# Constants as VectorE row sums, and a new order of the first loads, in a fused perceiver layer

## The chip, the cores and the metric

The kernel runs on one core of a Trainium2 chip, as one launch. The metric is the device time of one execution in microseconds. TensorE (PE) does the matrix products, VectorE (DVE), ScalarE (ACT) and GpSimd (POOL) work on rows, and SyncE (SP) issues nearly all transfers from HBM. The five engines run their own instruction lists in order and meet only at semaphores.

## The reference

For 16 sequences of 64 latent rows `x` (width 512) and 16 contexts of 1,601 key rows (width 384), all float32, one layer is computed:

```python
x = x + xattn(layernorm(x), ctx)      # one head, q = ln(x)Wq+bq, k = ln(ctx)Wk+bk, v = ln(ctx)Wv+bv, softmax, Wo, bo
x = x + attn(layernorm(x), ...)       # 16 heads of 32 on the 64 rows, relative positions
x = x + ffn(layernorm(x), ...)        # W1, W2 ternary by their mean magnitude, exact gelu, 2048 wide
```

Both layernorms of the cross attention have gains and offsets, so that its weights can be multiplied together ahead of the data.

## The kernel before

Two sequences share the 128 partitions, so there are 8 pairs. The work is a pipeline over steps `n`: in step `n` the cross attention of pair `n` is finished and the scores of pair `n+1` are made, self attention of pair `n-1` begins and of pair `n-2` ends. The feed-forward part follows behind all pairs. Every engine's list is written out by hand; what is placed earlier in a list is issued earlier, and a waiting instruction holds all behind it.

What matters here is the start, up to the first pair's output.

- **The fold.** Queries and keys need not be formed: `wqk` = Wq times Wk is made once by 16 products (line 744), 385 columns wide: 384 for the weights, one for the key offset. VectorE prepares the rows of Wk (lines 1212 to 1219), one block `e` of four after the other.
- **Constants.** A vector `TV` of 512 numbers (VectorE, lines 1266 to 1268) is multiplied by the prepared Wk on TensorE as 16 products of one column each (lines 1013 and 1015). `a_rows` (line 772) makes from the turned `x` what the keys are multiplied with; `scores` (line 824) does that for the four chunks 0, 1, tail (3) and 2 of a pair.
- **Key statistics.** VectorE's `key_stats` (line 1241) takes mean and variance of every key row from a second copy of the keys, `nat`, which comes in six loads of two tiles (0 to 5) and a tail of 65 rows. GpSimd raises them to the power of -1/2 (line 414), ScalarE spreads them (line 537), TensorE turns them (`key_factors`, line 797), VectorE multiplies scores by them and takes the maximum (line 1283, `exp_bias` up to line 1294), and ScalarE takes the exponentials (line 550).
- **The value side.** `value_product` makes Wv times Wo (`xwvo`, line 1031, three row blocks `m` of four products), `value_bias` (line 1048) makes a constant row from a vector `SV` (VectorE, lines 1420 and 1422) by four products, and `value_mean` (line 1040) the weighted mean row of `xwvo` by three. VectorE's `value_center` (line 1428) takes that mean off.
- **Weighted keys.** `turn_probs` (line 900), VectorE's `pt_scale` (line 1301) and `weighted` (line 914) go over 13 tiles of the pair. When a tile is used up, SyncE may load the next pair's `nat` into its place (line 274). The sum is turned (line 944), multiplied by `xwvo` (`xattn_o`, line 961) and added to `x` (`x1_sum`, line 1371); after the norm (`x1_norm`, line 1380) `y_turn` (line 1000) follows on TensorE, and then the last scores of the next pair.

On TensorE step 0 begins like this:

```python
                key_factors(p)
                if n == 0:
                    value_product()
                    value_bias()
```

and ends, between the weighted keys and the next pair's scores, with `value_mean()`. On VectorE the list after `exp_bias(0)` is `value_dots()`, `x_stats(1)` and `pt_scale(0, 0)`. On SyncE the first loads are followed by one quarter of the self-attention ("dense") weights `aw`, the next pair's keys and some rows; `step(0)` then waits for `value_bias` (line 348) and loads the other three quarters before any `nat` of pair 1.

Of the kernel before, what the change touches and what calls it, by code (L numbers as in the profile page):

```python
# [16 lines left out]
def build_program(nc, A, out):  # L17
# [25 lines left out]
    with ctx:  # L43
# [44 lines left out]
        wqk, at = carve(at, [P, KD, DC + 1])  # L88
# [14 lines left out]
        wkT, at = carve(at, [P, KE, DC + 1])  # L103
# [23 lines left out]
        xvo_bias, _ = carve(GS_AT + 4096, [P, D])  # L127
        rsk, at = carve(at, [P, H, L])
        ptT, at = carve(at, [P, HP, P])
# [137 lines left out]
        def _(sp):  # L267
# [61 lines left out]
            sp.dma_start(wo, A["wo"]).then_inc(s["wvo_loaded"], 16)  # L329
# [12 lines left out]
            def step(n):  # L342
                wms, following = magnitudes(n), magnitudes(n + 1)
                more = n + 1 < NT
                if n == 0:
                    sp.wait_ge(s["vbias_ps"], 1)
                    for i in range(1, 4):
                        sp.dma_start(aw[i], A["aw"][i]).then_inc(s["dense_loaded"], 16)
                for k in range(NG + 1):
                    if more:  # L350
                        load_nat(n + 1, k)
                    if k in (1, 3, NG) and (1, 3, NG).index(k) + 2 < len(wms):
                        load_wm(wms[(1, 3, NG).index(k) + 2])
                if n + 2 < NT:
                    load_x(n + 2)
# [149 lines left out]
        def _(act):  # L505
            act.wait_ge(s["vec_loaded"], 16)
            for c in range(KD):
                act.wait_ge(s["wqk_ps"], c + 1)
                act.activation(wqk[:, c, :], S[c][:, 0:DC + 1], ACT.Identity, bias=0.0, scale=col("xattn_ln1_g", c)).then_inc(s["wqk_ready"], 1)
# [22 lines left out]
            def spread_factors(p, g):  # L532
# [5 lines left out]
                         rs[p % 2][0:m, 8 * g:8 * g + 2 * n].unsqueeze(2).to_broadcast([m, 2 * n, L])).then_inc(s["factors_spread"], 1)  # L538

# [89 lines left out]
            yTx_out(0)  # L629
# [15 lines left out]
            def step(n):  # L645
# [6 lines left out]
                if n == 0:  # L652
                    for m in range(KC):
                        act.wait_ge(s["xvo_ps"], m + 1)
                        act.copy(xwvo[:, m, :], S[m]).then_inc(s["xvo_taken"], 1)
# [80 lines left out]
        def _(pe):  # L736
# [3 lines left out]
            for e in range(KE):  # L740
                pe.wait_ge(wq_loaded[e], 16)
                pe.wait_ge(s["k_ready"], e + 1)
                for c in range(KD):
                    ins = pe.matmul(S[c][:, 0:DC + 1], wqT[:, e, c * P:(c + 1) * P], wkT[:, e, :], start=(e == 0), stop=(e == KE - 1))
                    if e == KE - 1:
                        ins.then_inc(s["wqk_ps"], 1)
# [261 lines left out]

            x_turn(0)
            pe.wait_ge(s["t_ready"], 1)  # L1010
            for m in range(KC):
                for e in range(KE):
                    pe.matmul(W[0][:, m:m + 1], wkT[:, e, m * P:(m + 1) * P], sm(TV + e), start=(e == 0), stop=(e == KE - 1))
            for e in range(KE):
                ins = pe.matmul(W[0][:, KC:KC + 1], sm(TV + e).to_broadcast([P, P]), wkT[:, e, DC:DC + 1], start=(e == 0), stop=(e == KE - 1))
            ins.then_inc(s["const_ps"], 1)
            bias_max()
# [7 lines left out]
            def value_product():  # L1025
# [3 lines left out]
                for m in range(KC):  # L1029
# [4 lines left out]
            def value_mean():  # L1034

                pe.wait_ge(s["xvo_taken"], KC)
                pe.wait_ge(s["g2d_ready"], 1)
                pe.wait_ge(s["chunk_scaled"], 4)
                for m in range(KC):
                    ins = pe.matmul(S[3], sm(G2D + m).to_broadcast([P, P]), xwvo[:, m, :], start=(m == 0), stop=(m == KC - 1))  # L1040
                ins.then_inc(s["center_ps"], 1)

            def value_bias():

                pe.wait_ge(s["sv_ready"], 1)
                pe.wait_ge(s["chunk_scaled"], 1)
                for e in range(KE):
                    ins = pe.matmul(W[0][:, :], sm(SV + e).to_broadcast([P, P]), wo[:, e, :], start=(e == 0), stop=(e == KE - 1))
                ins.then_inc(s["vbias_ps"], 1)

            def step(n):
                p, t, r = stages(n)
                more = p + 1 < NT
                if t is not None:
                    q_rows(t)
                key_factors(p)
                if n == 0:
                    value_product()
                    value_bias()
# [8 lines left out]
                weighted(p, 1)  # L1068
                turn_probs(p, 3)
# [101 lines left out]
        def _(dve):  # L1171
            for u in range(2):
                dve.memset(st[u], 1.0).then_inc(s["padding_set"], 1)
            dve.wait_ge(s["rows_loaded"], 16)
# [93 lines left out]
            dve.tensor_tensor(sm(TV, KE), sm(TV, KE), col("xattn_bq", 0, KE), ALU.add).then_inc(s["t_ready"], 1)  # L1268
            dve.tensor_scalar(sm(KSC, KD), col("attn_bk", 0, KD), DH ** -0.5, None, ALU.mult).then_inc(s["ksc_ready"], 1)
# [145 lines left out]
            def value_dots():  # L1415
# [6 lines left out]
                dve.tensor_tensor(sm(SV, KE), sm(SV, KE), col("xattn_bv", 0, KE), ALU.add).then_inc(s["sv_ready"], 1)  # L1422

# [7 lines left out]
            def step(n):  # L1431
# [14 lines left out]
                if more:  # L1446
                    x_stats(p + 1)
                pt_scale(p, 0)
# [157 lines left out]
```

## Time and profile before

| what | us |
|---|---|
| median of three runs | 566.79 |
| the three runs | 562.96, 566.79, 568.53 |
| the profiled execution | 566.35 |
| its span, first to last instruction | 564.6 |

The span of the profiled execution is 1.75 us shorter than its time; the rest lies around it. All stages below are read in that one execution, in microseconds from the start of the span. A float32 product appears in the trace as two records, so that 16 products are "x32".

### The profile page before, as it was taken

What the parts mean: (1) busy time and instruction counts of PE and PEld (TensorE: products, weight loads), DVE (VectorE), ACT (ScalarE), POOL (GpSimd) and SP (SyncE); (2) the same over time, 40 slices, a digit from 0 to 9 for tenths busy, and PEclk for the clock granted to TensorE, in tenths of its full rate; (3) what the DMA queues carried; (4) which work ended last, traced back from release to release, by engine and by line L of the source; (5) the groups of instructions that cost most, each with busy time, mean ns of one, the idle gap of its engine ahead of it and who ended that gap; (6) DMA issues with size and microseconds to landing.
All of it is one profiled execution on the core that took longest, in us unless ns stands there. A gap on an engine that the chain in (4) does not pass through costs nothing.

```text
span 564.6 us, 10435 instructions
## 1 busy us (share of the span) xinstructions
PE 525.6 (93%) x4171; PEld 301.9 (53%) x4171; DVE 342.0 (61%) x765; ACT 196.1 (35%) x455; POOL 193.2 (34%) x132
## 2 busy tenths in 40 slices
PE   4979988987999989999998999999988879999996
PEld 2834446553765845666484575656574334444442
DVE  6754185373768468377575836967596895435333
ACT  0233014433723541653373255145143542211110
POOL 0141213224316233440721524269364991000000
PEclk9989999998999999999999999999999989999999
DMA  8999895498499789959959986853527420002002
GB/s 278 424 375 423 330 357 217 184 343 274 174 390 245 276 301 236 324 204 367 262 208 391 202 330 227 241 184 154 113 75 192 145 74 1 1 0 75 0 2 75
DMA packets 42096, 122.45 MB, mean 217 GB/s; under 512 B 19640, under 2 KB 21432, under 8 KB 37312
## 3 DMA queue, kind: packets, MB, share of 16 engines
q1 hardware_dynamic: 24256, 109.20, 53.5%
q10 hardware_dynamic: 17792, 12.58, 9.6%
q8 instruction: 33, 0.54, 0.4%
q14 instruction: 15, 0.12, 0.1%
HBM read 111.29 MB, written 10.49 MB: 216 GB/s over the span
## 4 chain that ended last, share of the span: by engine, by line
PE 61%; DVE 11%; DMA 8%; issue 8%; POOL 5%; ACT 4%; SPq 2%; ACTq 0%; DVEq 0%; POOLq 0%
PE u_ps L914 11%; PE s_ps L1147 9%; PE w_ps L1132 8%; DMA area<-in_kt_dram 6%; PE s_ps L824 6%; PE u_ps L835 5%; PE w_ps L937 5%; POOL area L414 2%; PE w_ps L846 2%; PE w_ps L928 2%; DVE area L1241 2%; PE s_ps L1031 2%; DMA area<-in_nat_dram 2%; PE w_ps L900 1%; DVE area L1325 1%
## 5 line engine op out<-in xcount | busy, mean ns | idle before, releaser
L1241 DVE BATCH_NORM_STATS2 area<-area 128x6 f32<-128x384 f32 (+1 forms) x208 | 99.7, 546 | 26.8 <-DMA area<-in_nat_dram 26.8
L824 PE MATMUL s_ps<-area 128*64 128x512 f32 (+1 forms) x384 | 72.8, 522 | 5.8 <-DMA area<-in_kt_dram 4.8
L914 PE MATMUL u_ps<-area 128*64 128x384 f32 (+1 forms) x416 | 72.4, 491 | 1.2 <-DVE area L1301 1.2
L1147 PE MATMUL s_ps<-area 128*128 128x512 f16 x256 | 61.7, 385 | 4.8 <-DVE area L1520 4.8
L1132 PE MATMUL w_ps<-area 128*128 128x512 f16 x256 | 60.7, 378 | 0.2 <-ACT area L724 0.2
L449 POOL TENSOR_SCALAR area<-area 128x512 f16<-128x512 f32 x32 | 55.6, 1753 | 15.0 <-DMA area<-in_wf_dram 15.0
L414 POOL TENSOR_TENSOR area<-area 128x16 f32<-128x16 f32 (+1 forms) x16 | 39.0, 2438 | 46.6 <-DVE area L1256 46.6
L1283 DVE CUSTOM_DVE_ANT_0 area<-w_ps,area 128x512 f32<-128x512 f32 x24 | 15.4, 690 | 58.6 <-PE w_ps L797 51.8
L724 ACT ACTIVATE area<-w_ps,area 128x512 f32<-128x512 f32 x32 | 22.0, 686 | 79.5 <-PE w_ps L1132 74.0
L824 PEld LDWEIGHTS s_ps<-area 128*64 128x64 f32 x384 | 24.1, 139 | 44.9 <-issue 40.6
L914 PEld LDWEIGHTS u_ps<-area 128*64 128x64 f32 (+1 forms) x416 | 27.6, 135 | 34.2 <-issue 29.5
L1147 PEld LDWEIGHTS s_ps<-area 128*128 128x128 f16 x256 | 24.9, 98 | 37.1 <-DVE area L1520 5.8
L419 POOL TENSOR_TENSOR area<-area 128x1 f32<-128x1 f32 x16 | 9.3, 583 | 92.7 <-DVE area L1363 92.7
L1132 PEld LDWEIGHTS w_ps<-area 128*128 128x128 f16 x256 | 24.3, 96 | 31.1 <-issue 1.0
L1301 DVE TENSOR_TENSOR area<-w_ps,area 128x512 f32<-128x512 f32 (+1 forms) x32 | 18.7, 588 | 34.7 <-PE w_ps L900 34.7
L1518 DVE TENSOR_SCALAR area<-area 128x512 f16<-128x512 f32 x24 | 11.7, 488 | 44.8 <-ACT area L724 44.8
L391 POOL TENSOR_TENSOR area<-area 128x1 f32<-128x1 f32 x8 | 4.4, 553 | 86.0 <-DVE area L1229 86.0
L835 PEld LDWEIGHTS u_ps<-area 128*128 128x128 f32 x256 | 29.2, 191 | 6.7 <-issue 5.7
L835 PE MATMUL u_ps<-area 128*128 128x128 f32 x256 | 30.7, 277 | 0.7 <-ACT area L622 0.7
L846 PE MATMUL w_ps<-area 128*128 128x128 f32 x256 | 30.6, 277 | 0.0
L937 PE MATMUL w_ps<-area 128*128 128x512 f32 x64 | 29.3, 600 | 0.7 <-ACT area L580 0.7
L1412 DVE SCALAR_TENSOR_TENSOR area<-area 128x512 f16<-128x512 f32 x32 | 26.5, 869 | 4.8 <-PE u_ps L914 3.2
(169 smaller groups left out, 835.9 us busy)
## 6 DMA issues: line engine op xcount, KB each, us to landing
area<-in_nat_dram SPq DMA_DIRECT2D x48, 768.0 KB, 10.3
area<-in_kt_dram SPq DMA_DIRECT2D x24, 1536.0 KB, 7.8
area<-in_wf_dram SPq DMA_DIRECT2D x32, 256.0 KB, 8.2
skew<-area ACTq DMA_DIRECT2D x8, 1024.0 KB, 8.6
area<-in_wf_dram SPq DMA_DIRECT2D x16, 512.0 KB, 3.4
area<-in_aw_dram SPq DMA_DIRECT2D x4, 1024.0 KB, 9.3
area<-skew ACTq DMA_DIRECT2D x16, 256.0 KB, 12.2
area<-in_x_dram SPq DMA_DIRECT2D x8, 256.0 KB, 10.2
```

Of the source, the lines that this page charges most:

```text
L414: pool.tensor_tensor(rs[p % 2][:, sl], ve[:, sl], minus_half[:, 0:sl.stop - sl.start], ALU.pow).then_inc(s["rs_ready"], 1)
L449: pool.tensor_scalar(wneg[f % 4][:, w, :], wraw[f % 4][:, w, :], sm(WNTHR + w), None, ALU.is_lt).then_inc(s["neg_done"], 1)
L724: act.activation(gf[i % 2], HID[i % 2][:, :], ACT.Gelu, bias=col("ffn_b1", i % KF), scale=1.0).then_inc(s["gelu_done"], 1)
L824: ins = pe.matmul(S[ch][u * L:(u + 1) * L, 0:n], a_sb[:, c, u * L:(u + 1) * L], x[:, u, c, :], start=(c == 0), stop=(c == KC - 1))
L835: ins = pe.matmul(U[:, m * P:(m + 1) * P], awq[:, c, m * P:(m + 1) * P], yT[:, c, :], start=(c == 0), stop=(c == KD - 1))
L846: ins = pe.matmul(W[0][:, m * P:(m + 1) * P], awk[:, c, m * P:(m + 1) * P], yT[:, c, :], start=(c == 0), stop=(c == KD - 1))
L914: ins = pe.matmul(U[u * L:(u + 1) * L, 0:DC], pT[g % 2][0:m, i, u * L:(u + 1) * L], nat[0:m, j, u, :], start=(j == 0), stop=(j == NJ - 1))
L937: ins = pe.matmul(dst[:, :], ctxT[:, c, :], awo[:, c, :], start=(c == 0), stop=(c == KD - 1))
L1132: ins = pe.matmul(HID[i % 2][:, :], wf16[:, f, 0, c * P:(c + 1) * P], zt[:, 4 * h:4 * h + 4, z, c, :], start=(k == 0), stop=(k == 2 * KD - 1))
L1147: ins = pe.matmul(S[q], g[i % 3][:, q * P:(q + 1) * P], wf16[:, f, 1, :], start=(f == 0 and z == 0), stop=(f == KF - 1 and z == 1))
L1241: dve.bn_stats(st[b][0:m, 2 * j + u, :], nat[0:m, j, u, :]).then_inc(s["key_stats"], 1)
L1412: dve.scalar_tensor_tensor(out=wf16[:, f, w, :], in0=wraw[f % 4][:, w, :], scalar=sm(WTHR + w), in1=wneg[f % 4][:, w, :], op0=ALU.is_gt, o ...
```

## The change

**Sums on VectorE.** The constants, the value bias and the value mean are matrix-vector products whose weights lie on the partitions. Before, TensorE did them in 16, four and three products. Now VectorE multiplies each block by its column of numbers and adds the blocks up (one TENSOR_SCALAR and then SCALAR_TENSOR_TENSORs, each of which waits for the one before), and TensorE sums the one resulting tile over the partitions by a product with ones: four products of one column, one of 512 and one of 512. The three sums lie in `rsk`, which self attention uses later.

**Order on TensorE and ScalarE.** `x` is turned ahead of the fold's last block; two of the three value blocks are made ahead of `key_factors`, the third behind; `value_bias` stands behind the weighted tiles 4 to 7. ScalarE turns out `x` first, takes all four score chunks before it spreads factors, and takes two value blocks out between the first and second half of the factors.

**Order on SyncE.** The first pair's transposed keys `kt` come ahead of most of their second form `nat`; the value weights come ahead of the last `nat`; the three quarters of the dense weights come behind pair 1's `nat`.

**Width.** The fold is 386 columns wide, with one column of zeros (one small memset).

```diff
@@ SyncE, first loads
-            for k in range(2):
-                load_nat(0, k)
             load_kt(0, 0)
+            load_nat(0, 0)
+            load_kt(0, 1)
+            load_nat(0, 1)
+            load_kt(0, NCH)
+            load_kt(0, 2)
             for k in range(2, 4):
                 load_nat(0, k)
-            load_kt(0, 1)
+            sp.dma_start(wvT, A["wvT"]).then_inc(s["wvo_loaded"], 16)
+            sp.dma_start(wo, A["wo"]).then_inc(s["wvo_loaded"], 16)
             for k in range(4, NG + 1):
                 load_nat(0, k)
-            load_kt(0, NCH)
-            load_kt(0, 2)
             load_x(1)
-            sp.dma_start(wvT, A["wvT"]).then_inc(s["wvo_loaded"], 16)
-            sp.dma_start(wo, A["wo"]).then_inc(s["wvo_loaded"], 16)
@@ SyncE, step(0): this block moves behind the loop over load_nat(n + 1, k)
                 if n == 0:
                     sp.wait_ge(s["vbias_ps"], 1)
                     for i in range(1, 4):
                         sp.dma_start(aw[i], A["aw"][i]).then_inc(s["dense_loaded"], 16)
@@ ScalarE
+            act.wait_ge(s["x_turned"], 1)
+            act.copy(yTx.rearrange("p a b -> p (a b)"), W[2][:, :]).then_inc(s["yTx_out"], 1)
...
             scores_out(0, 0)
             key_offset_sums(0)
+            for ch in ORDER[1:]:
+                scores_out(0, ch)
             spread_factors(0, 0)
             spread_factors(0, 1)
-            for ch in ORDER[1:]:
-                scores_out(0, ch)
+            for m in range(KC - 1):
+                value_out(m)
             spread_factors(0, 2)
             spread_factors(0, 3)
@@ TensorE
+            for e in range(KE - 1):
+                fold_qk(e)
             x_turn(0)
-            pe.wait_ge(s["t_ready"], 1)
+            fold_qk(KE - 1)
+            bias_max()
+            pe.wait_ge(s["t_ready"], KE + 1)
             for m in range(KC):
-                for e in range(KE):
-                    pe.matmul(W[0][:, m:m + 1], wkT[:, e, m * P:(m + 1) * P], sm(TV + e), start=(e == 0), stop=(e == KE - 1))
+                pe.matmul(W[0][:, m:m + 1], const_sum[:, m * P:(m + 1) * P], ones_f[:, 0:1], start=True, stop=True)
...
-                for m in range(KC):
-                    ins = pe.matmul(S[3], sm(G2D + m).to_broadcast([P, P]), xwvo[:, m, :], start=(m == 0), stop=(m == KC - 1))
-                ins.then_inc(s["center_ps"], 1)
+                pe.matmul(S[3], ones_f, mean_sum, start=True, stop=True).then_inc(s["center_ps"], 1)
...
+                if n == 0:
+                    value_product(range(KC - 1))
                 key_factors(p)
                 if n == 0:
-                    value_product()
-                    value_bias()
+                    value_product(range(KC - 1, KC))
...
                 weighted(p, 1)
+                if n == 0:
+                    value_bias()
@@ VectorE, end of value_dots(); value_means() is alike, over KC blocks of xwvo, each behind its xvo_taken
+                dve.wait_ge(s["sv_ready"], 1)
+                dve.tensor_scalar(bias_sum, wo[:, 0, :], sm(SV), None, ALU.mult).then_inc(s["sv_ready"], 1)
+                for e in range(1, KE):
+                    dve.wait_ge(s["sv_ready"], e + 1)
+                    dve.scalar_tensor_tensor(out=bias_sum, in0=wo[:, e, :], scalar=sm(SV + e), in1=bias_sum, op0=ALU.mult,
+                                             op1=ALU.add).then_inc(s["sv_ready"], 1)
@@ VectorE, step(0)
                 if more:
                     x_stats(p + 1)
+                if n == 0:
+                    value_means()
                 pt_scale(p, 0)
```

On SyncE, the first loads behind the weights. Before (`in_kt` 128x3072 is one key chunk, the last of them chunk 2; `in_nat` two tiles of the second form; `in_wvT` and `in_wo` the value weights):

```order
L316 DMA area<-in_b1row_dram 128x512
L274 DMA area<-in_nat_dram 128x1536 x2
L292 DMA area<-in_kt_dram 128x3072
L274 DMA area<-in_nat_dram 128x1536 x2
L292 DMA area<-in_kt_dram 128x3072
L274 DMA area<-in_nat_dram 128x1536 x2
L276 DMA area<-in_nat_tail_dram 65x768
L282 DMA area<-in_kt_tail_dram 128x390
L286 DMA area<-in_kt_dram 128x3072
L296 DMA area<-in_x_dram 128x512
L328 DMA area<-in_wvT_dram 128x1536
L329 DMA area<-in_wo_dram 128x2048
```

The same place on SyncE now:

```order
L320 DMA area<-in_b1row_dram 128x512
L296 DMA area<-in_kt_dram 128x3072
L278 DMA area<-in_nat_dram 128x1536
L296 DMA area<-in_kt_dram 128x3072
L278 DMA area<-in_nat_dram 128x1536
L286 DMA area<-in_kt_tail_dram 128x390
L290 DMA area<-in_kt_dram 128x3072
L278 DMA area<-in_nat_dram 128x1536 x2
L329 DMA area<-in_wvT_dram 128x1536
L330 DMA area<-in_wo_dram 128x2048
L278 DMA area<-in_nat_dram 128x1536 x2
L280 DMA area<-in_nat_tail_dram 65x768
```

The last key chunk stood behind all `nat` and now stands behind two of the seven; the last `nat` loads stood ahead of the value weights and now stand behind them.

On VectorE, from the end of `value_dots` to the first `pt_scale` of pair 0. Before:

```order
L1420 ISA area 128x1
L1422 TENSOR_TENSOR area<-area 128x4 [waits k_dot]
L1224 BN_STATS area<-area 128x6 [waits x_loaded1]
L1227 BN_AGGR area<-area 128x2 [waits xs_normed,xs_stats]
L1229 TENSOR_SCALAR area<-area 128x1 [waits xs_moments]
L1301 TENSOR_TENSOR area<-w_ps,area 128x512 [waits pt_turned] x2
```

Now (L1438 and L1440 are `value_dots`, L1319 is `pt_scale`):

```order
L1438 ISA area 128x1
L1440 TENSOR_TENSOR area<-area 128x4 [waits k_dot]
L1442 TENSOR_SCALAR area<-area 128x512 [waits sv_ready]
L1445 SCALAR_TENSOR_TENSOR area<-area 128x512 [waits sv_ready] x3
L1236 BN_STATS area<-area 128x6 [waits x_loaded1]
L1239 BN_AGGR area<-area 128x2 [waits xs_normed,xs_stats]
L1241 TENSOR_SCALAR area<-area 128x1 [waits xs_moments]
L1452 TENSOR_SCALAR area<-area 128x512 [waits xvo_taken,g2d_ready]
L1456 SCALAR_TENSOR_TENSOR area<-area 128x512 [waits g2d_ready,xvo_taken] x2
L1319 TENSOR_TENSOR area<-w_ps,area 128x512 [waits pt_turned] x2
```

Seven instructions over whole rows now stand ahead of the first `pt_scale`.

On TensorE, around the key factors of pair 0. Before (L824 is `scores`, L797 `key_factors`, L1031 `value_product`, L1048 `value_bias`, L900 `turn_probs`):

```order
L824 MATMUL s_ps<-area 64x512 x6
L797 MATMUL w_ps<-area 128x128 x12
L797 MATMUL s_ps<-area 128x65
L1031 MATMUL s_ps<-area 128x512 x12
L1048 MATMUL w_ps<-area 128x512 x4
L900 MATMUL w_ps<-area 128x128 x8
```

Now (L837 is `scores`, L1044 `value_product`, L810 `key_factors`, L913 `turn_probs`):

```order
L837 MATMUL s_ps<-area 64x512 x6
L1044 MATMUL s_ps<-area 128x512 x8
L810 MATMUL w_ps<-area 128x128 x12
L810 MATMUL s_ps<-area 128x65
L1044 MATMUL s_ps<-area 128x512 x4
L913 MATMUL w_ps<-area 128x128 x8
```

Eight of the twelve value products moved ahead of the key factors, and the four products of `value_bias` are gone from this place.

## Rows read from the trace of the kernel before

**Rows 1.** Chain of waits, 0 to 140: start us, us, what (x records)

```profile
11.94 26.82 DMA area<-in_kt_dram
38.89 4.45 PE s_ps L824 x12
...
61.82 10.26 DMA area<-in_nat_dram
...
74.05 1.96 DVE area L1428 x3
...
89.59 2.73 PE s_ps L824 x12
```

**Rows 2.** DMA issues of one moment: engine, count, KB, us to landing

```profile
area<-in_wo_dram SPq DMA_DIRECT2D x1, 1024.0 KB, 23.8
```

**Rows 3.** Timeline of SyncE: start us, us, issue

```profile
19.95 1.57 SPq L329 DMA_DIRECT2D area<-in_wo_dram  x1
```

**Rows 4.** Timeline of TensorE: start us, us, out<-in, shape, x records [idle before]

```profile
7.54 13.10 PE L744 MATMUL s_ps<-area 128*128 128x385 f32 x32 [1.48 <-DVE area L1219]
...
20.91 2.74 PE L1013 MATMUL w_ps<-area 128*128 128x1 f32 x24
...
45.07 10.53 PE L1031 MATMUL s_ps<-area 128*128 128x512 f32 x24
...
69.95 2.85 PE L1040 MATMUL s_ps<-area 128*128 128x512 f32 x6
...
88.93 0.66 PE L1000 MATMUL w_ps<-area 128*128 128x128 f32 x4 [2.11 <-DVE area L1380]
```

**Rows 5.** Windows: length, PE, PEld, DVE, ACT, POOL busy, granted clock, DMA share, GB/s

```profile
36.00:37.00 1.00, 0.00 (x0) 0.00 (x0) 0.89 (x5) 0.88 (x3) 0.00 (x0) 1.00 1.02 408
40.00:41.00 1.00, 1.00 (x4) 0.30 (x2) 0.00 (x0) 0.00 (x0) 0.00 (x0) 0.50 1.02 422
```

**Rows 6.** Timeline of VectorE

```profile
15.21 1.15 DVE L1266 CUSTOM_DVE_ANT_0 area<-area 128x512 f32<-128x512 f32 x1
...
33.65 2.86 DVE L1241 BATCH_NORM_STATS2 area<-area 128x6 f32<-128x384 f32 x6 [0.32 <-DMA area<-in_nat_dram]
...
37.03 0.17 DVE L1256 SCALAR_TENSOR_TENSOR area<-area 128x10 f32<-128x10 f32 x1
...
46.61 0.21 DVE L1294 TENSOR_SCALAR area<-area 128x1 f32<-128x1 f32 x1
...
49.14 0.16 DVE L1422 TENSOR_TENSOR area<-area 128x4 f32<-128x4 f32 x1
...
50.16 0.15 DVE L1229 TENSOR_SCALAR area<-area 128x1 f32<-128x1 f32 x1
...
59.52 1.29 DVE L1301 TENSOR_TENSOR area<-w_ps,area 128x512 f32<-128x512 f32 x2 [9.21 <-PE w_ps L900]
...
85.86 0.67 DVE L1371 TENSOR_TENSOR area<-area,w_ps 128x512 f32<-128x512 f32 x1
```

**Rows 7.** VectorE by line and shape, whole span: count | busy us, mean ns | idle

```profile
L1380 DVE TENSOR_SCALAR area<-area 128x512 f32<-128x512 f32 x8 | 4.3, 541 | 2.2 <-POOL area L419 2.2
L1202 DVE TENSOR_SCALAR area<-area 128x2 f32<-128x2 f32 x1 | 2.4, 2386 | 0.0
L1428 DVE SCALAR_TENSOR_TENSOR area<-area,s_ps 128x512 f32<-128x512 f32 x3 | 2.1, 741 | 0.0
```

**Rows 8.** Timeline of GpSimd

```profile
15.06 2.08 POOL L394 TENSOR_SCALAR area<-area 128x512 f32<-128x512 f32 x1
...
37.28 1.96 POOL L414 TENSOR_TENSOR area<-area 128x10 f32<-128x10 f32 x1 [2.17 <-DVE area L1256]
```

**Rows 9.** Timeline of ScalarE and TensorE at the last key factors

```profile
43.84 0.81 ACT L537 COPY area<-area 128x512 f32<-128x512 f32 x2
44.52 0.66 PE L797 MATMUL w_ps<-area 128*128 128x128 f32 x4 [0.16 <-ACT area L537]
```

**Rows 10.** VectorE's line 1266: ns min/median/max, first and last start

```profile
L1266 DVE CUSTOM_DVE_ANT_0 area<-area x4: 693/693/1151, 14.5 to 17.1; 128x512 f32<-128x512 f32 x4
```

More of the change, by code:

```diff
@@ L127, in build_program @@
         xvo_bias, _ = carve(GS_AT + 4096, [P, D])
+        RSK_AT = at
         rsk, at = carve(at, [P, H, L])
+        const_sum, _ = carve(RSK_AT, [P, DC + 2])
+        mean_sum, _ = carve(RSK_AT, [P, D])
+        bias_sum, _ = carve(RSK_AT + 4 * D, [P, D])
         ptT, at = carve(at, [P, HP, P])
@@ L353, in step @@
                         load_wm(wms[(1, 3, NG).index(k) + 2])
+                if n == 0:
+                    sp.wait_ge(s["vbias_ps"], 1)
+                    for i in range(1, 4):
+                        sp.dma_start(aw[i], A["aw"][i]).then_inc(s["dense_loaded"], 16)
                 if n + 2 < NT:
@@ L1023, in _, with value_product @@
                 scores(0, ch)
-            def value_product():
+            def value_product(ms):
                 pe.wait_ge(s["wvo_loaded"], 32)
                 pe.wait_ge(s["scores_taken"], 4)
-                for m in range(KC):
+                for m in ms:
                     for e in range(KE):
@@ L1034, in value_mean @@
             def value_mean():
[L1036 to L1037 removed]
+                pe.wait_ge(s["g2d_ready"], KC + 1)
                 pe.wait_ge(s["chunk_scaled"], 4)
[L1039 to L1041 removed]
+                pe.matmul(S[3], ones_f, mean_sum, start=True, stop=True).then_inc(s["center_ps"], 1)
             def value_bias():
[L1045 removed]
+                pe.wait_ge(s["sv_ready"], KE + 1)
                 pe.wait_ge(s["chunk_scaled"], 1)
[L1047 to L1049 removed]
+                pe.matmul(W[0][:, :], ones_f, bias_sum, start=True, stop=True).then_inc(s["vbias_ps"], 1)
             def step(n):
@@ L1268, in _ @@
             dve.tensor_tensor(sm(TV, KE), sm(TV, KE), col("xattn_bq", 0, KE), ALU.add).then_inc(s["t_ready"], 1)
+            dve.wait_ge(s["t_ready"], 1)
+            dve.tensor_scalar(const_sum, wkT[:, 0, :], sm(TV), None, ALU.mult).then_inc(s["t_ready"], 1)
+            for e in range(1, KE):
+                dve.wait_ge(s["t_ready"], e + 1)
+                dve.scalar_tensor_tensor(out=const_sum, in0=wkT[:, e, :], scalar=sm(TV + e), in1=const_sum, op0=ALU.mult,
+                                         op1=ALU.add).then_inc(s["t_ready"], 1)
             dve.tensor_scalar(sm(KSC, KD), col("attn_bk", 0, KD), DH ** -0.5, None, ALU.mult).then_inc(s["ksc_ready"], 1)
@@ L1422, in value_dots, with value_means @@
                 dve.tensor_tensor(sm(SV, KE), sm(SV, KE), col("xattn_bv", 0, KE), ALU.add).then_inc(s["sv_ready"], 1)
+                dve.wait_ge(s["sv_ready"], 1)
+                dve.tensor_scalar(bias_sum, wo[:, 0, :], sm(SV), None, ALU.mult).then_inc(s["sv_ready"], 1)
+                for e in range(1, KE):
+                    dve.wait_ge(s["sv_ready"], e + 1)
+                    dve.scalar_tensor_tensor(out=bias_sum, in0=wo[:, e, :], scalar=sm(SV + e), in1=bias_sum, op0=ALU.mult,
+                                             op1=ALU.add).then_inc(s["sv_ready"], 1)
+            def value_means():
+                dve.wait_ge(s["g2d_ready"], 1)
+                dve.wait_ge(s["xvo_taken"], 1)
+                dve.tensor_scalar(mean_sum, xwvo[:, 0, :], sm(G2D), None, ALU.mult).then_inc(s["g2d_ready"], 1)
+                for m in range(1, KC):
+                    dve.wait_ge(s["xvo_taken"], m + 1)
+                    dve.wait_ge(s["g2d_ready"], m + 1)
+                    dve.scalar_tensor_tensor(out=mean_sum, in0=xwvo[:, m, :], scalar=sm(G2D + m), in1=mean_sum, op0=ALU.mult,
+                                             op1=ALU.add).then_inc(s["g2d_ready"], 1)
             def value_center():
```

29 lines of the change are left out of this document (13 added, 16 removed).

## The prediction

> **What bounds the kernel now.** I read the chain of waits first, since it names what each stage ends on. The change touches only the first 90 of 564.6 us, and there the chain has five pieces [rows 1]. Up to 38.8 it is the queue of loads: chunk 2 of the first pair's keys is issued at 11.94 and lands 26.8 later. From there to 59.5 it is TensorE: scores, key factors, value products and value bias. From 61.8 to 72.1 it is a load again, pair 1's first `nat`, which stands behind three quarters of the dense weights. Then VectorE works without a break, over `value_center` (73.96 to 75.92 in its own timeline, 74.05 in the chain), to `x1_sum` at 85.86 [rows 1, 6]. TensorE then waits 2.11 for the norm and starts `y_turn` at 88.93 [rows 4]. Whatever is gained in the start must show as an earlier `y_turn`; from 89.6 on the list is unchanged [rows 1].
>
> TensorE's share for the whole span says little here. The clock says more: an idle engine at 36 to 37 and again up to 38.9 is followed by a granted clock of 0.50, the lower level of 1.2 GHz, at 40 to 41 [rows 5], and the twelve score records there take 4.45, against 2.73 for the same twelve at 89.59 [rows 1]. That idle time thus costs 1.72 more.
>
> **Front end: faster, and hidden.** The fold takes 13.10 for 32 records [rows 4]; one more column of 386 is under 0.3% of that, 0.03 us, and I count nothing either way. The one-column products fall from 32 records to 8; the 24 of line 1013 take 2.74 [rows 4], 0.114 each, so 24 fewer save 2.7 us. Chunk 2 is no longer late: it ends 9,049 KB of the queue, and before, 9,622 KB (up to `nat` 4) had landed by 33.65, when `nat` 5 came in [rows 6]. At 36 TensorE had done the other three chunks and was idle [rows 5]; 2.7 off and chunk 2's 2.73 [rows 1] on, all scores are done by 36, instead of 43.3. This looks like 7 us, but nothing waits for scores alone: the key factors need the `nat` statistics, and the value products need `wo`. Both are late next.
>
> **Loads.** The sizes are 384 KB for the gains and offsets, 768 and 1,024 for Wk and Wq, 21.5 for the small vectors, 256 each for `x` and the offsets' row, 1,536 a key chunk, 195 a tail, 768 a `nat`, 768 for `wvT`, 1,024 for `wo`. Before, `wo` ends 14,364 KB at 19.95 + 23.8 = 43.75 [rows 2, 3], and chunk 2 ends 12,316 KB at 38.76 [rows 1]: 2,048 KB in 4.99, 410 KB a us. Now `wo` ends 12,377 KB, so it lands at 38.9, and `nat` 5 ends 13,913 KB, so it lands at 43.75 - 451/410 = 42.65, 9.0 later than its 33.65 [rows 6].
>
> **From `nat` 5 to the exponentials.** Each step is taken from where it stood before. VectorE's last statistics: 33.65 to 37.20, 3.55 [rows 6], so 46.2. GpSimd's power: from there to 37.28 + 1.96 = 39.24, 2.04 [rows 8], so 48.24. ScalarE's spread to TensorE's third group: 43.84 to 44.52, 0.68 [rows 9], so 48.92. From there to the end of `exp_bias`: 44.52 to 46.82, 2.30 [rows 6, 9], so 51.22 instead of 46.82. The two early value blocks hide behind this: eight products of 10.53/12 = 0.88 [rows 4] are 7.0 from 38.9, and 1.7 more if the clock dips after the idle time before them, which ends at 47.6, 1.3 before the third group could start. That cover is gone if `wo` lands more than 1.3 later than I say. The last value block, four products, runs from 49.6 to 53.1 beside the exponentials.
>
> **The new wait.** Before, TensorE was busy with value products and the value bias, and VectorE waited 9.21 for the first turned probabilities [rows 6]. Now TensorE has turned the first two groups of probabilities by 54.3 and waits for `pt_scale`, which stands behind this on VectorE.
>
> First `value_dots`, from 46.82 to 49.30: 2.48 [rows 6].
>
> Second `bias_sum`, new: one TENSOR_SCALAR of 0.54 and three SCALAR_TENSOR_TENSORs of 0.74 [rows 7], with some 0.05 between dependent ones: 2.9. No row shows this form with both inputs in SBUF and float32 out; line 1428 reads one from PSUM. From below it is not under the 0.54 of the one-input form, from above not over 1.15, the slowest of the four whole-row products of line 1266, which read two inputs from SBUF [rows 10]. I take 0.74, the same operation; it is also near the median of line 1266, 0.69.
>
> Third `x_stats`, from the end of `value_dots` to the end of line 1229 at 50.31: 1.0 [rows 6].
>
> Fourth the mean's three, new: 0.54 + 2 x 0.74 + 0.1 = 2.1. Beside them GpSimd norms pair 1's `x`, released by `x_stats`. The one row of such an overlap is line 1266 at 15.21: with GpSimd's norm of 2.08 from 15.06 [rows 8] it took 1.15 where the median of its line is 0.69 [rows 6, 10]. I add 0.46.
>
> That is 8.9 behind 51.22: `pt_scale` at 60.1, against 59.52 [rows 6], 0.6 late. The range of the five two-input rows (0.54 to 1.15) moves it from 0.4 early to 2.7 late.
>
> TensorE has then been idle for 6 us, twice what preceded the dip at 40, so I expect the dip here too: 1.72, and in this stage TensorE is the bound. The weighted stage also takes in the one product of `value_bias`, 0.95 (a third of line 1040's 2.85 [rows 4]), and `value_mean` falls from three products to one, which saves 1.9. `value_mean`, which ended at 69.95 + 2.85 = 72.80, therefore ends at 72.80 + 0.6 + 1.7 + 0.95 - 1.9 = 74.15.
>
> **To `y_turn`.** Pair 1's `nat` no longer stands behind the dense weights; its first tile is issued 0.6 behind the 61.82 of before [rows 1], near 62.4, into a queue that is empty by then and lands before 70 (a load of 768 KB is 1.9 at 410 KB a us). VectorE does its statistics after `pt_scale` and then waits for `value_mean`, so `value_center` starts at 74.15 against 73.96, and everything behind it, `x1_sum` and `y_turn` too, is 0.2 late. The dense weights are issued near 74 and take 3,072/410 = 7.5; q of pair 0 needs them behind the last scores, after 92, so they cost nothing. On SyncE they stand ahead of pair 2's first keys, which the next step uses.
>
> The sum on the profiled execution of 566.35 is +0.2, so 566.6. It lies 0.44 below the median of the runs shown, so the forecast is no change against either. In short: the 7 us won in front are eaten by `nat` 5 being 9.0 later and by seven rows on VectorE where it was not the bound.
>
> **Rivals.** First, no clock dip. Then `value_mean` ends at 72.45 and `value_center` starts 1.5 earlier than before: 564.9. For it: the dip needs an idle engine, and TensorE's 2.11 before `y_turn` brought none, as the next scores take 2.73 [rows 1, 4]. Against it: 6 us are longer than both.
>
> Second, the row sums are hidden. If VectorE were through by the time TensorE has turned the probabilities, `pt_scale` would start 2.9 + 2.1 + 0.46 earlier than 60.1, at 54.7, 4.8 before the old time and without a dip: 4.8 + 1.9 - 0.95 = 5.75 earlier on TensorE. TensorE's own list before `y_turn` ends at 88.93 - 2.11 = 86.82, so it would be ready at 81.1, and the norm would be done at 82.0 (`value_center` at 67.05, then 11.9 to `x1_sum` and 3.07 from there to `y_turn`, both as before [rows 4, 6]): 6.9 earlier, 559.4. It needs the sums to cost nothing, which rows of 0.74 each speak against; or `nat` 5 to land 4 us earlier than its place in the queue, for which nothing speaks.
>
> Third, slower: VectorE is shut out by GpSimd. The place is the mean's rows, the mechanism a wait to the end of GpSimd's norm. Line 1202, a row of two elements, took 2.39 [rows 7]. If the last mean row waits out the norm of 2.08 [rows 8] instead of 0.46, `pt_scale` is 1.6 later still: 568.2. It decides as soon as the norm begins before the last mean row, which is nearly sure, since it is released 0.7 after `x_stats` and the rows last 2.1. Against it: the row at 15.21 began inside the norm and did not wait for its end. By the Trainium skill, "SBUF — State Buffer", section "Who interferes with whom", an instruction of VectorE with two SBUF inputs and one of GpSimd that reads SBUF take a shared pair of ports in turn, each for its whole length; that is this rival, and by it the time would be 568.2. The row at 15.21 does not bear it out in full, line 1202 does.
>
> Fourth, slower too: `wo` keeps its old landing of 43.75, because transfers do not end in the order of the queue. Eight products then end at 52.4 and push the third group 3.5 later: 570.1. All landings read so far are in order.
>
> **Chances.** Forecast 0.50, first rival (no dip) 0.20, second (hidden sums) 0.08, third (ports) 0.15, fourth (`wo`) 0.07. A measurement of this kernel can tell about 1%, 5.7 us, from no change. Around the median of 566.79 only the second rival gets below 561.1, and only the fourth with another late step above 572.5: faster 0.08, same 0.88, slower 0.04. The runs before spread from 4 below to 2 above their median, and the first and third rivals lie at 564.9 and 568.2: the range is 562.0 to 569.5, and leaves out the second and the fourth.
>
> **What would show it.** Right: all scores done by 36 and nothing gained by it; `nat` 5's statistics starting near 42.7; TensorE idle from about 54 to 60 before the first weighted tile, and a clock of 0.5 shortly after; `pt_scale` at 59.5 to 61; `value_center` waiting for the mean, not for a load. Wrong: `pt_scale` before 57, twelve weighted records at full clock, or a `y_turn` more than 3 us away from 88.9.

## The result, and the profile after

| kernel | us, median (range, runs) | ratio to before, 95% interval |
|---|---|---|
| before | 566.22 (562.96 to 568.53, 4) | |
| after | 557.61 (556.62 to 560.80, 4) | 0.9858 [0.9816, 0.9901] |

The change is 8.6 us faster; the forecast was 566.6 and no change. The profiled execution of after took 557.74, its span 556.0 (before 566.35 and 564.6). In after's listing `weighted` is L927, `value_product` L1044, `value_bias` L1057, `value_mean` L1051, `y_turn` L1013, `pt_scale` L1319, the bias rows L1442 and L1445, the mean rows L1452 and L1456, `value_center` L1463.

TensorE's timeline of after, the rows that answer to [rows 4] and to the forecast's stages:

```profile
26.77 8.31 PE L837 MATMUL s_ps<-area 128*64 128x512 f32 x48
36.52 7.15 PE L1044 MATMUL s_ps<-area 128*128 128x512 f32 x16 [1.44 <-DMA area<-in_wo_dram]
...
47.65 1.11 PE L810 MATMUL w_ps<-area 128*128 128x128 f32 x4 [3.11 <-ACT area L543]
...
48.67 6.26 PE L1044 MATMUL s_ps<-area 128*128 128x512 f32 x8
54.77 1.03 PE L913 MATMUL w_ps<-area 128*128 128x128 f32 x8
59.88 4.50 PE L927 MATMUL u_ps<-area 128*64 128x384 f32 x16 [4.08 <-DVE area L1319]
...
64.90 2.80 PE L927 MATMUL u_ps<-area 128*64 128x384 f32 x16
...
72.17 1.13 PE L1051 MATMUL s_ps<-area 128*128 128x512 f32 x2
...
88.32 0.66 PE L1013 MATMUL w_ps<-area 128*128 128x128 f32 x4 [1.00 <-DVE area L1398]
```

VectorE's and GpSimd's timelines of after, for [rows 6] and [rows 8]:

```profile
41.35 2.86 DVE L1253 BATCH_NORM_STATS2 area<-area 128x6 f32<-128x384 f32 x6 [1.00 <-DMA area<-in_nat_dram]
...
50.19 0.21 DVE L1312 TENSOR_SCALAR area<-area 128x1 f32<-128x1 f32 x1
...
52.92 0.49 DVE L1442 TENSOR_SCALAR area<-area 128x512 f32<-128x512 f32 x1
53.44 2.33 DVE L1445 SCALAR_TENSOR_TENSOR area<-area 128x512 f32<-128x512 f32 x3
55.69 0.69 DVE L1236 BATCH_NORM_STATS2 area<-area 128x6 f32<-128x512 f32 x1
...
56.71 0.49 DVE L1452 TENSOR_SCALAR area<-area 128x512 f32<-128x512 f32 x1
57.30 1.93 DVE L1456 SCALAR_TENSOR_TENSOR area<-area 128x512 f32<-128x512 f32 x2
59.15 1.27 DVE L1319 TENSOR_TENSOR area<-w_ps,area 128x512 f32<-128x512 f32 x2
...
73.34 2.06 DVE L1463 SCALAR_TENSOR_TENSOR area<-area,s_ps 128x512 f32<-128x512 f32 x3 [2.30 <-PE s_ps L1051]
...
57.71 2.29 POOL L398 TENSOR_SCALAR area<-area 128x512 f32<-128x512 f32 x1
```

And the clock behind TensorE's idle time (windows, columns as in [rows 5]):

```profile
61.00:62.00 1.00, 1.00 (x6) 0.49 (x4) 0.00 (x0) 0.00 (x0) 0.00 (x0) 0.50 0.00 0
```

These rows are the forecast's start, a little early throughout: scores done by 35.1 and nothing gained by it, `wo` late next, then `nat` 5, then `pt_scale` behind seven row sums while TensorE is idle from 55.8 to 59.9, then the half clock. `y_turn` starts 0.6 earlier than before [rows 4]. The 8.6 us are not here. Starts of like instructions in the two timelines show where they come in:

| place | before | after | shift |
|---|---|---|---|
| `y_turn`, pair 0 | 88.93 | 88.32 | -0.6 |
| `y_turn`, pair 1 | 132.78 | 132.34 | -0.4 |
| `y_turn`, pair 2 | 183.15 | 180.53 | -2.6 |
| context turn, step 3 | 211.67 | 207.49 | -4.2 |
| context turn, step 5 | 307.11 | 301.09 | -6.0 |
| feed-forward product | 456.81 | 450.68 | -6.1 |
| end of span | 564.6 | 556.0 | -8.6 |

Two of the jumps are stalls on TensorE of which the kernel before has two and the kernel after none. TensorE's timeline of before at steps 3 and 5, and the page's row of an instruction queue:

```profile
208.39 0.91 PE L888 MATMUL s_ps<-area 32*64 32x64 f32 x64
209.24 0.86 PE L862 MATMUL w_ps<-area 64*32 64x64 f32 x64
211.67 0.55 PE L944 MATMUL u_ps<-area 128*128 128x128 f32 x3 [1.56 <-issue]
...
302.49 1.09 PE L991 MATMUL w_ps<-area 128*128 128x128 f32 x8
303.52 0.91 PE L888 MATMUL s_ps<-area 32*64 32x64 f32 x64
304.37 0.80 PE L862 MATMUL w_ps<-area 64*32 64x64 f32 x56
306.86 0.32 PE L862 MATMUL w_ps<-area 64*32 64x64 f32 x8 [1.70 <-issue]
...
q8 instruction: 33, 0.54, 0.4%
```

and of after at step 3:

```profile
205.85 0.91 PE L901 MATMUL s_ps<-area 32*64 32x64 f32 x64
206.70 0.86 PE L875 MATMUL w_ps<-area 64*32 64x64 f32 x64
207.49 0.55 PE L957 MATMUL u_ps<-area 128*128 128x128 f32 x3
```

"issue" is time in which nothing the profile shows is waited for, and one stall lies in the middle of 64 products with no wait between them. The other jumps: pair 2's scores (-2), one feed-forward product at half clock in before and not in after (-1.4), and the last store: the span ends 2.6 behind VectorE's last row instead of 3.6 (-1.0).

### The profile page after: what moved, and what is told of

It reads as the page before. It is cut to its first block, busy times and chain, and to the rows that moved or that the text cites. A ratio compares the mean times of both kernels' runs of the same rounds, so it can differ in the third digit from the quotient of the medians.

```text
span 556.0 us, 10383 instructions
## 1 busy us (share of the span) xinstructions
PE 517.0 (93%) x4137; PEld 295.8 (53%) x4137; DVE 349.0 (63%) x777; ACT 196.4 (35%) x455; POOL 193.7 (35%) x132
## 4 chain that ended last, share of the span: by engine, by line
PE 58%; DVE 14%; DMA 8%; issue 7%; POOL 5%; ACT 4%; SPq 3%; ACTq 0%; DVEq 0%; POOLq 0%
PE u_ps L927 12%; PE s_ps L1158 9%; PE w_ps L1143 8%; DMA area<-in_nat_dram 6%; PE u_ps L848 5%; PE s_ps L837 5%; PE w_ps L950 4%; DVE area L1253 3%; POOL area L418 2%; PE w_ps L859 2%; PE w_ps L941 2%; DMA area<-in_kt_dram 2%; PE w_ps L913 1%; DVE area L1343 1%; DVE area L1301 1%
## 5 line engine op out<-in xcount | busy, mean ns | idle before, releaser
L927 PE MATMUL u_ps<-area 128*64 128x384 f32 (+1 forms) x416 | 74.1, 500 | 5.0 <-DVE area L1319 5.0
L837 PE MATMUL s_ps<-area 128*64 128x512 f32 (+1 forms) x384 | 69.2, 503 | 2.4 <-DMA area<-in_kt_dram 1.3
L1158 PE MATMUL s_ps<-area 128*128 128x512 f16 x256 | 60.2, 378 | 4.8 <-DVE area L1557 4.8
L453 POOL TENSOR_SCALAR area<-area 128x512 f16<-128x512 f32 x32 | 55.8, 1760 | 15.3 <-DMA area<-in_wf_dram 15.3
L927 PEld LDWEIGHTS u_ps<-area 128*64 128x64 f32 (+1 forms) x416 | 27.9, 137 | 39.2 <-issue 30.8
L837 PEld LDWEIGHTS s_ps<-area 128*64 128x64 f32 x384 | 23.2, 136 | 40.0 <-issue 35.4
L1319 DVE TENSOR_TENSOR area<-w_ps,area 128x512 f32<-128x512 f32 (+1 forms) x32 | 18.7, 588 | 28.1 <-PE w_ps L913 28.1
```

Of the source, the lines that this page charges most:

```text
L453: pool.tensor_scalar(wneg[f % 4][:, w, :], wraw[f % 4][:, w, :], sm(WNTHR + w), None, ALU.is_lt).then_inc(s["neg_done"], 1)
L837: ins = pe.matmul(S[ch][u * L:(u + 1) * L, 0:n], a_sb[:, c, u * L:(u + 1) * L], x[:, u, c, :], start=(c == 0), stop=(c == KC - 1))
L927: ins = pe.matmul(U[u * L:(u + 1) * L, 0:DC], pT[g % 2][0:m, i, u * L:(u + 1) * L], nat[0:m, j, u, :], start=(j == 0), stop=(j == NJ - 1))
L1158: ins = pe.matmul(S[q], g[i % 3][:, q * P:(q + 1) * P], wf16[:, f, 1, :], start=(f == 0 and z == 0), stop=(f == KF - 1 and z == 1))
```

## Experiments

**The theories.** Place of the code: each record of a product is counted as two machine instructions (weights and product; the page has 4,171 of each before and 4,137 after), a wait that stands alone as one. The sums took 34 records out (24 of the constants, 6 of the value bias, 4 of the mean) and put one wait in. Everything behind step 0 thus stands 2 x 34 - 1 = 67 instructions earlier in the code. The instruction queue's 33 packets of 0.54 MB are 16 KB each; twice 4,171 instructions are 253 to a packet, waits not counted, and the programs below with 47 or 64 products more show 34 packets. If code is loaded in such pieces, a piece that holds nothing but small products is used up before the next is there, and a shift by 67 puts the border elsewhere. The rival: the stalls, or the rest of the 8.6, come from the run or from the new order itself.

**Both kernels again, unchanged.**

> The kernel before, once more, for a second profile. The 8.6 us between the two profiles arise behind 130 us, in code that the change does not touch: two idle times of TensorE of 1.56 and 1.70 that nothing in the profile released (211.67 and 306.86), a half clock at 135 to 139 and one at 457 to 460. Theory A (they belong to the kernel: the idle times to where its TensorE code is cut into loads, the clock to the length of idle times that its schedule has): all four come back at the same places within 0.3 us, 564 to 567 us. Theory B (chance of one run): at least two of the four are gone or elsewhere.

> The changed kernel, once more. Theory A: again no idle time of TensorE without a releaser, full clock at the last scores of step 1 (twelve records in 2.80) and at 450 us, 556 to 559 us. Theory B: one or more of the four turn up here, each 1.4 to 2 us, 559 to 563 us.

Before: 565.09, with both stalls (1.89 and 0.82). After: 562.03, with none. But pair 2's part did not repeat: in this run of after, `y_turn` of pair 2 starts at 184.35, later than in either run of before, behind a load of keys 2.12 late and twelve score records at half clock (4.42). From pair 1's to pair 2's `y_turn` it is 49.9 to 50.9 in the six traces of before and its shifted forms, and 48.2, 51.6 and 50.4 in three of after: those 2 us belong to the run.

**The place alone, in both directions.** 17 products of one column (four instructions each, one fewer in all) ahead of TensorE's first transpose, where it waits anyway, put after's later code where before's stands; 47 of them put before's where after's stands (modulo 256, to within 2).

```diff
             pe.wait_ge(s["ident_ready"], 1)
+            for _ in range(17):
+                pe.matmul(U[0:1, P + 2:P + 3], ident_f[:, 0:1], ones_f[:, 0:1], start=True, stop=True)
             pe.wait_ge(s["b1_step"], 1)
```

> The changed kernel with 17 products of one column and one row ahead of the first transpose, in time that TensorE idles anyway. They put every later TensorE instruction at the place in its code that it has in the kernel before. If the idle times without a releaser come from where the code is cut into loads (theory A), both come back, behind the products of lines 864 to 877 of steps 3 and 5, 1.6 and 1.7 us: 3.3 to 3.6 us slower than the changed kernel, near 561. If they come from the time at which transfers happen to lie (theory B), they stay away: 557 to 558.

> The kernel before with 47 such small products ahead of its first transpose, which put its later TensorE instructions at the place that they have in the changed kernel, up to two, counted from the start of a load of code. Theory A: both idle times without a releaser vanish, 3.3 to 3.6 us faster than before, near 562.8; the half clocks at 135 and 457 may stay. Theory B: no change, ratio 1.000 within 0.003.

After at before's place: 566.07 (561.16 to 569.13), ratio 0.9982 [0.9952, 1.0012]. Both stalls are back:

```profile
210.58 0.86 PE L877 MATMUL w_ps<-area 64*32 64x64 f32 x64
213.45 0.55 PE L959 MATMUL u_ps<-area 128*128 128x128 f32 x3 [2.01 <-issue]
...
308.18 0.79 PE L877 MATMUL w_ps<-area 64*32 64x64 f32 x56
310.67 0.32 PE L877 MATMUL w_ps<-area 64*32 64x64 f32 x8 [1.70 <-issue]
```

Before at after's place: 563.16, ratio 0.9955 [0.9925, 0.9986], and no such stall. At before's place, then, the change is worth nothing that can be measured, and products that compute nothing make the kernel before faster.

**Is it the place modulo 256?** 64 products move the code by 256 instructions less one; 8 move it by 31.

> The kernel before with 64 products of one column ahead of the first transpose: 64 x 4 = 256 instructions less one, so all code behind them stands where it stands in the kernel before, modulo 256, though 47 products freed it of the stalls. If the place modulo 256 decides: both 'issue' stalls are back at the same products as in the kernel before (step 3 at the first context turn or within a record of it, step 5 with 7 or 8 of the 64 attention-value products left), 0.8 to 2.0 us each, ratio 0.997 to 1.003. If the tiny products themselves helped in the earlier run (a warmer start, code further off), 64 help as 47 did: no stall, ratio about 0.9955.

> The kernel before with 8 products of one column ahead of the first transpose, 32 instructions less one. If TensorE's code comes in pieces of 256 instructions (128 records) whose borders stand fixed, each 'issue' stall moves ahead by 16 records in the list, to where no semaphore and no line of the program changes: step 3 to between the 48th and 49th of its 64 attention-value products (now behind the 64th), step 5 to between the 40th and 41st (now behind the 56th). Its length is 0.5 to 2.0 us, since the piece used up ahead of it is still nearly all small products. If the stall belongs to a place in the program, it stays where it was.

With 64, 565.35, ratio 0.9972 [0.9937, 1.0007], and the stalls are back at the same products. The ratio alone could not tell this from the 0.9955 with 47; the trace does:

```profile
211.14 0.49 PE L946 MATMUL u_ps<-area 128*128 128x128 f32 x3 [1.36 <-issue]
...
305.75 0.32 PE L864 MATMUL w_ps<-area 64*32 64x64 f32 x8 [0.53 <-issue]
```

With 8, one run of 563.74, there was no stall at all, where 0.5 to 2.0 was expected: a miss for the size, though the stall did leave its place. The length has to be reckoned from when the piece begins. In step 3 of before the used-up piece is exactly lines 888 and 862: 1.71 us, and the next was there 3.28 after its start. With 8 products the piece begins 31 instructions earlier, in slower products of 0.14 to 0.18 us a record, and lasts some 3.9 us (an estimate from those rows), so the next would be there in time. This was found after the fact; the same estimate was then stated ahead of a run with 2 products:

> The kernel before with 2 products of one column ahead of the first transpose, 8 instructions less one. The run with 8 products showed no stall, so what is looked for is stated more closely here. A piece of 256 instructions that holds both runs of small products and nothing else is used up in 1.7 us (208.39 to 210.10 in the kernel before); the piece behind it was there 3.1 to 3.7 us after that in step 3 of the runs so far, and 3.2 to 4.4 us in step 5, where the piece begins 8 slower products earlier. If the stall is that difference, it falls now between the 60th and the 61st of step 3's 64 attention-value products (give or take one), and is shorter by the 0.45 us that 7 more instructions of slower products take: 0.9 to 1.6 us; in step 5 between the 52nd and 53rd, 0 to 1.1 us. If the border is not at a fixed place modulo 256: the stall stays behind the 64th and 56th product, or is gone in both steps.

```profile
207.67 1.09 PE L993 MATMUL w_ps<-area 128*128 128x128 f32 x8
208.69 0.92 PE L890 MATMUL s_ps<-area 32*64 32x64 f32 x64
209.54 0.83 PE L864 MATMUL w_ps<-area 64*32 64x64 f32 x60
212.01 0.30 PE L864 MATMUL w_ps<-area 64*32 64x64 f32 x4 [1.64 <-issue]
...
304.21 0.92 PE L890 MATMUL s_ps<-area 32*64 32x64 f32 x64
305.07 0.86 PE L864 MATMUL w_ps<-area 64*32 64x64 f32 x64
```

The border fell where it was reckoned, behind the 60th product record; the stall, 1.64, is just over the 0.9 to 1.6 given, and step 5 has none. (The one run took 564.51.)

**The change without its sums, at both places.** The three sums are products on TensorE again; the order of loads, scores and value blocks stays.

```diff
-                pe.wait_ge(s["sv_ready"], KE + 1)
+                pe.wait_ge(s["sv_ready"], 1)
                 pe.wait_ge(s["chunk_scaled"], 1)
-                pe.matmul(W[0][:, :], ones_f, bias_sum, start=True, stop=True).then_inc(s["vbias_ps"], 1)
+                for e in range(KE):
+                    ins = pe.matmul(W[0][:, :], sm(SV + e).to_broadcast([P, P]), wo[:, e, :], start=(e == 0), stop=(e == KE - 1))
+                ins.then_inc(s["vbias_ps"], 1)
...
```

(The same for the constants and the mean. The first expectation miscounts: it is 16 products for the constants and 3 for the mean.)

> The changed kernel, but the three sums are again products on TensorE (20 small ones for the constants, 4 for the value bias, 4 for the mean); the new order of loads, scores and value product stays. Its code behind step 0 then stands one instruction off the place it has in the kernel before. Place of the code: both 'issue' stalls are back (about 1.6 and 1.7 us, near 212 and 307) and the time is 564 to 567 us, ratio 0.996 to 1.002. If the new order of the start gave the gain by itself: no more than 561 us whatever the place of the code. Up to the first y_turn the time should be within 1.5 us of the changed kernel's 88.3, since pt_scale starts some 3 us earlier and TensorE then pays six more products of 512 columns (about 5 us, less the dip that the earlier start may spare).

> As the run without the sums, with 47 products of one column ahead of the first transpose, in which TensorE waits anyway: this puts the code behind step 0 within one instruction (modulo 256) of its place in the changed kernel. Place of the code: neither 'issue' stall, 559 to 563 us, ratio 0.988 to 0.995, some 3 to 4 us below the run without these products. If the sums themselves gave the gain: 565 to 567 us as without them.

At before's place: 561.44 (560.09 to 564.69), ratio 0.9928 [0.9902, 0.9953], with both stalls, now behind the 63rd and the 55th record instead of the 64th and 56th, as its one instruction more wants:

```profile
54.80 2.80 PE L927 MATMUL u_ps<-area 128*64 128x384 f32 x16 [1.36 <-DVE area L1321]
...
206.92 0.21 PE L875 MATMUL w_ps<-area 64*32 64x64 f32 x1 [1.32 <-issue]
...
300.21 0.78 PE L875 MATMUL w_ps<-area 64*32 64x64 f32 x55
302.38 0.32 PE L875 MATMUL w_ps<-area 64*32 64x64 f32 x9 [1.39 <-issue]
```

At after's place: 559.41 (557.66 to 560.00), ratio 0.9875 [0.9849, 0.9901], no stall. Here the expectation failed for the first kernel, in its time: with the stalls it is still 4.5 us below before. The new order is worth that much, and VectorE's sums give part of it back (1.7 to 3.1, see below). `pt_scale` starts at 54.07 without the sums, against 57.83 in the trace of after taken beside it (59.15 in the first); `y_turn` of pair 0 comes at 85.85, against 86.63.

**After once more, beside it; and the mean's rows later.** The second kernel moves `x_stats(1)` and `value_means()` on VectorE; TensorE's list is after's.

> The changed kernel as it is, to size its gain beside the other runs of this call. Place of the code (TensorE's code is 67 instructions shorter ahead of step 0, and neither run of small products uses up one load of code by itself): 558 to 562 us, ratio 0.986 to 0.993, no idle 'issue' of TensorE at the context turn of step 3 or in the attention values of step 5. If the gain of the first measurement was mostly a lucky start of the clock, the ratio is 0.995 or more.

> The changed kernel, with the statistics of the second pair's x rows and the sums for the mean (1.0 and 2.5 us on VectorE) moved behind the first two pt_scale instructions; TensorE's list is as in the changed kernel. If this new wait holds TensorE back as forecast: the first pt_scale starts at 55.7 instead of 59.15, weighted starts at 56.4 after under 1 us of idle instead of 4.08, the half clock of 61 to 64 is gone (up to 1.7 us more), y_turn comes 3 to 5 us earlier than 88.3, and the time is 3 to 5 us below the changed kernel's of the same call. If the key statistics and their loads set y_turn anyway: y_turn moves by under 1 us, and so does the time.

```diff
-                if more:
+                if more and n:
                     x_stats(p + 1)
-                if n == 0:
-                    value_means()
                 pt_scale(p, 0)
...
                 reciprocal(p)
+                if n == 0:
+                    x_stats(1)
+                    value_means()
```

After: 561.09 (558.52 to 561.97), ratio 0.9905 [0.9878, 0.9931]. This interval meets the first one only between 0.9878 and 0.9901, so the first median was somewhat lucky. With the mean's rows later: 556.27 (552.21 to 558.09), ratio 0.982 [0.9788, 0.9852], the best kernel of the study and 4.8 us below after. Its TensorE and VectorE:

```profile
55.46 2.80 PE L927 MATMUL u_ps<-area 128*64 128x384 f32 x16 [1.55 <-DVE area L1319]
...
82.20 0.66 PE L1013 MATMUL w_ps<-area 128*128 128x128 f32 x4 [1.00 <-DVE area L1398]
...
54.72 1.28 DVE L1319 TENSOR_TENSOR area<-w_ps,area 128x512 f32<-128x512 f32 x2
...
57.19 0.49 DVE L1452 TENSOR_SCALAR area<-area 128x512 f32<-128x512 f32 x1
57.78 1.94 DVE L1456 SCALAR_TENSOR_TENSOR area<-area 128x512 f32<-128x512 f32 x2
```

Against the trace of after taken beside it, TensorE's idle ahead of the weighted keys falls from 5.01 to 1.55, its first weighted group from 4.13 to 2.80, and `y_turn` comes at 82.20 instead of 86.63.

**The parts side by side** (each ratio is to runs of before taken beside it; differences times 566):

| | at before's place, with stalls | at after's place, without | place |
|---|---|---|---|
| before | 1.000 | 0.9955 | -2.5 us |
| new order, sums on TensorE | 0.9928 | 0.9875 | -3.0 us |
| new order, sums on VectorE (after) | 0.9982 | 0.9905 | -4.4 us |
| the same, mean's rows later | not run | 0.982 | |

Read downwards, the order gives 4.1 or 4.5 us, the sums take back 3.1 or 1.7, and their later place brings 4.8. Each ratio is uncertain by some 0.3%, 1.7 us, and a difference of two by more, so the spread between columns says nothing.

## Why the prediction was wrong

**The step that failed** is "from 89.6 on the list is unchanged", with "whatever is gained in the start must show as an earlier `y_turn`": the sum has nothing for all that lies behind. The order of the list is unchanged, but its place in the code is not, and the place costs 3.3 us in the profiled run of before (1.56 + 1.70) and 2.5 to 4.4 by the ratios. That the place does it is shown both ways: the stalls come to after with 17 idle products, leave before with 47, come back with 64, and move by the counted records with 2. That code loaded in pieces is behind it is argued from these counts and from the queue's packets. The two "issue" stalls stood in the trace of before; the prediction did not ask what they were.

**Right: the start.** With the place held the change measured 0.9982 [0.9952, 1.0012], 1.0 us less, between 2.7 less and 0.7 more; the forecast was +0.2 us. The start need have no part in that 1.0: `y_turn` of pair 0 starts at 88.86 in this run's trace, and between 87.61 and 89.20 in the six of before and its shifted forms, and the last store's 1.0 is in this trace too. Point by point: scores by 36 (35.1); `nat` 5 at 42.65 (41.35, as `wo` landed by 36.5 and not 38.9, so the queue ran ahead of 410 KB a us); the third group of key factors at 48.92 (47.65); `exp_bias` at 51.22 (50.40); `bias_sum` 2.9 (52.92 to 55.69: 2.8); the mean with its overlap 2.56 (56.71 to 59.15: 2.4); `pt_scale` at 60.1 (59.15); the dip of 1.72 (4.50 against the 2.80 of the next such group, at 64.90: 1.70); `value_center` at 74.15, waiting for the mean (73.34, `<-PE L1051`); `y_turn` at 89.1 (88.32). The error of 0.8 to 1.3 is that of the loads, carried through. One term was off without a price: the last value block took 6.26 and not 3.5, at a granted clock of 0.50 from 49 to 53, so TensorE was idle for 4.08 ahead of the weighted keys and not for 6.

**The rivals.** No dip: refuted, the clock was 0.50. Hidden sums: not so in after. With the mean's rows later it nearly comes true: `pt_scale` forecast at 54.7 (54.72), `y_turn` at 82.0 (82.20). The first agreement is luck: that run still has the 2.8 of `bias_sum` ahead of `pt_scale`, no longer the 1.0 of `x_stats`, and `exp_bias` ended 1.8 before the forecast (49.43). From `pt_scale` to `y_turn` the rival's working holds: 27.5, forecast 27.3. Shut out by GpSimd: refuted in its price. In the chain of waits of after the two mean rows stand apart:

```profile
57.30 0.76 DVE area L1456
58.16 1.07 DVE area L1456
```

The second, which began inside GpSimd's norm, took 0.31 more than the first, not 2.08 more, and the norm 2.29 instead of 2.08 [rows 8]: each lost a few tenths. The Trainium skill, "SBUF — State Buffer", section "Who interferes with whom", calls the shared ports an exclusive lock, by which one would wait for the end of the other; these rows do not show that. Line 1202 of before, the prediction's example, does: it ends with the GpSimd row that began beside it (377.24 and 377.22).

```profile
374.85 2.39 DVE L1202 TENSOR_SCALAR area<-area 128x2 f32<-128x2 f32 x1
374.85 2.37 POOL L425 TENSOR_TENSOR area<-area 128x1024 f32<-128x1024 f32 x1
```

So such a wait exists in this kernel, but the mean's rows did not meet it. `wo` at its old landing: refuted, it landed earlier than forecast.

**What stays open.** Of the first comparison's 8.6 us, pair 2's scores (about 2) came with the run. The last store's 1.0 did not: the span ends 3.6 behind VectorE's last row in all six traces of before and its shifted forms, 2.5 to 2.6 in all five with the sums on VectorE, and 3.3 in the two with the sums back on TensorE. Why is open; the prediction had nothing for it. A feed-forward stretch of about one product at half clock (1.4 in before) occurs in all six traces of before and its shifted forms, and of after's forms in the two with idle products ahead, not in the other five; why was not tried. In the traces it lies, beside the stalls, in the 4.4 us between after's two places.

## What to carry to other kernels

An edit that changes how many instructions an engine has moves all its later code, and where that code runs through many short instructions, the place alone can be worth as much as the edit: look for "issue" stalls in the trace first, and compare at equal places (a few idle products at the start will do) before an edit is credited. A sum moved to another engine is free only where that engine isn't waited for: the mean's rows, with the statistics of the next `x`, cost 4.8 us ahead of the first two `pt_scale` instructions, against the same rows behind them. When a forecast says "unchanged from here on", check the idle time without a releaser behind that point too.

## What was unexpected of the hardware

**Code that is late.** By this count, in the runs with a stall, the next piece of TensorE's code was there 3.1 to 3.8 us after the piece before it had begun in step 3 (six traces: 3.28 in before, 208.39 to 211.67), and 3.2 to 4.4 in step 5 (five traces: 4.37 in before, 302.49 to 306.86), while 256 instructions of small products last 1.7 us. The transfer queues were full then, as in before's windows around the first stall:

```profile
210.00:211.00 1.00, 0.11 (x10) 0.00 (x0) 1.00 (x4) 0.65 (x2) 0.00 (x0) 1.00 1.02 412
211.00:212.00 1.00, 0.33 (x3) 0.34 (x4) 1.00 (x2) 0.00 (x0) 0.00 (x0) 1.00 0.94 389
```

Whether it would be quicker with empty queues was not tried. The Trainium skill, "Runtime: NRT & Kernel Launch", section "Instruction fetch mechanics", gives blocks of 256 instructions, the next fetched while the one at hand runs; the shifts by 2 and 64 products agree. It calls the cost of a border mostly hidden; here the two borders cost 3.3 us of 564.6.

**The clock after short idle times.** Idle of much the same length did and did not bring the half clock: ahead of pair 2's keys, twelve score records took 4.49 after 1.85 of idle in the third trace of after, and 2.80 after 1.86 in the kernel with the later mean, each with 1.33 of idle ahead of the `y_turn` before it. What decides it is not shown by these rows.
